# A four-layer graph network on one core: the last layer's edge pass as a walk over edge groups and node blocks, and another order of fronts in the projections

## The reference, cut to what matters

```
hn  = relu(layernorm(x))                      # the same norm ahead of every layer
msg = (hn @ weight[r] + bias[r])[src]         # r = edge type, 0 to 3
agg = segment_max(msg, dst, 6250)             # a node without edges gets 0
x   = x + agg + hn @ weight[4] + bias[4]
```

## Time and profile before

| | before |
|---|---|
| median of 3 runs | 5873.08 us |
| profiled execution | 5876.16 us, span 5874.4 us |
| PE busy | 3278.1 us (56%) |
| DVE | 2906.4 us (49%) |
| ACT | 1827.9 us (31%) |
| POOL | 3903.4 us (66%) |
| mean granted clock of TensorE | 0.728 |
| the last edge pass, first gather to the end of the span | 4816.0 to 5874.4 |
| of it behind the last scanned chunk | 5804 to 5874.4 |

### The profile page before, as it was taken

One profiled execution on the slowest core, in us unless ns is written; L12 is line 12 of the kernel. 1 busy time (PEld: TensorE's weight loads), 2 busy tenths in 40 slices (PEclk: granted clock), 3 DMA queues, 4 the chain that ended last, 5 costly groups with the idle time before them and its releaser, 6 DMA issues. The chain is left out here.

```text
span 5874.4 us, 89970 instructions
## 1 busy us (share of the span) xinstructions
PE 3278.1 (56%) x15772; PEld 2756.8 (47%) x15773; DVE 2906.4 (49%) x7625; ACT 1827.9 (31%) x6493; POOL 3903.4 (66%) x4083
## 2 busy tenths in 40 slices
PE   3444555545555525889999894244555563334332
PEld 3444455444555523677777644233445533333331
DVE  4233344434455656788888852344555652222221
ACT  2111111111122213666666653233344441111110
POOL 4777777677777747777776003777777517777776
PEclk9667777766677756999999995566677785555555
DMA  4222222211111112344444211222222134444443
GB/s 122 61 62 63 63 65 66 72 53 52 53 53 52 53 41 78 111 113 117 119 117 113 95 46 31 52 53 54 53 53 52 38 111 130 133 132 130 131 133 107
DMA packets 441899, 474.71 MB, mean 81 GB/s; under 512 B 131954, under 2 KB 337214, under 8 KB 441695
## 3 DMA queue, kind: packets, MB, share of 16 engines
q0 software_dynamic: 130464, 264.37, 17.1%
q1 hardware_dynamic: 184116, 146.31, 8.3%
q10 hardware_dynamic: 127227, 63.09, 3.6%
HBM read 315.46 MB, written 157.97 MB: 81 GB/s over the span
## 5 line engine op out<-in xcount | busy, mean ns | idle before, releaser
L1194 PE MATMUL pa<-arena,weighted 128*128 x4480 | 860.0, 367 | 855.8 <-POOLq L913 511.2
L1194 PEld LDWEIGHTS pa<-arena,weighted 128*128 128x128 f32 x4480 | 795.4, 273 | 909.4 <-issue 909.2
L422 POOL DMA_INDIRECT arena<-y_tab,slot x784 | 739.8, 944 | 398.7 <-issue 209.4
L1607 POOL DMA_INDIRECT arena<-t_tab,src_idx x784 | 777.5, 992 | 265.7 <-issue 216.0
L919 POOL DMA_INDIRECT arena<-h_tab,src_idx x784 | 742.8, 947 | 308.1 <-issue 221.9
L2490 POOL DMA_INDIRECT arena<-t_tab,src_idx x784 | 753.3, 961 | 244.9 <-issue 224.6
L919 POOL DMA_INDIRECT arena<-sage_tab,src_idx x784 | 739.8, 944 | 262.4 <-issue 216.1
L471 DVE TENSOR_TENSOR_SCAN scan_t<-mask,scan_t,pa 128x512 f32<-128x512 bf16 x196 | 250.9, 1280 | 737.1 <-PE pa L495 737.1
L495 PE MATMUL pa<-ident,arena 128*128 128x128 f32 x784 | 218.3, 434 | 603.9 <-DMA arena<-y_tab,slot 603.9
L495 PEld LDWEIGHTS pa<-ident,arena 128*128 128x128 f32 x784 | 140.1, 217 | 681.9 <-DMA arena<-y_tab,slot 430.8
L2731 PE MATMUL pa<-weighted 128*128 128x130 f32 x2240 | 422.6, 364 | 21.0 <-ACT weighted L2809 11.0
(11 more groups left out here) (522 smaller groups left out, 6559.9 us busy)
## 6 DMA issues: line engine op xcount, KB each, us to landing
gat_tab<-out_rows SPq DMA_DIRECT2D x248, 260.0 KB
scan_rows<-out_rows ACTq DMA_DIRECT2D x196, 256.0 KB, 3.7
arena<-t_tab,src_idx POOLq DMA_INDIRECT x1568
mask<-cut_row SPq DMA_DIRECT2D x196, 128.0 KB, 3.1
arena<-h_tab,src_idx POOLq DMA_INDIRECT x784
arena<-sage_tab,src_idx POOLq DMA_INDIRECT x784
y_tab<-arena SPq DMA_DIRECT2D x49, 256.0 KB, 2.3
arena<-y_tab,slot POOLq DMA_INDIRECT x784, 2.8
```

The source lines that it names most:

```text
L422: nc.gpsimd.indirect_dma_start(out=rows(c, t), out_offset=None, in_=table[:, :], in_offset=bass.IndirectOffsetOnAxis(ap=slot[:, c, t:t + 1 ...
L1194: ins = nc.tensor.matmul(pa[:, b * CE:b * CE + RW], hot[b][:, t * P:(t + 1) * P], ring[:, bass.ds(start + t * RW, RW)], start=(t == 0), st ...
L1607: nc.gpsimd.indirect_dma_start(out=rows[:, g % QR * QT + t, :], out_offset=None, in_=t1_tab[:, :], in_offset=bass.IndirectOffsetOnAxis(ap= ...
```

## The change

**The last pass** becomes a walk of the same 160 steps. `edge_pass`, `gather_results`, `scan_rows`, `last_idx`, `slot` and the rows of zeros go. POOL gathers by group into the ring of 8 groups, straight from `y_idx`; a group's slot is free when its last step has been staged. Tables in the pass's head: SP reads the destinations, DVE multiplies dst + 1 with the flag of each node's last edge (`last`), SP writes this to `last_rows`, POOL fetches it by step after group 2 (two gathers of 128 rows of 896), and PE and DVE turn it into a new `rel`, in which an edge is zero or negative unless it is the last of its node in the step's block. Then for step s, with b = s % 2:

- ACT `stage_group`: copy the 7 tiles out of the ring; `load_mask`: DMA of the cuts of the group to all partitions
- PE `turn`: 7 transposes; DVE `scan` over 896 edges, and two single-column operations for the carry (if the next step has the same group, the carry stays as it was, else it is the last column)
- PE `back`: 7 transposes; ACT `keep_back`: copy of 896 columns
- DVE `build`: one-hot of last edges; PE `select`: 7 products of `hot` with the kept rows, summed in PSUM, which pick each node's last row or zero
- DVE `add` to the block's rows of x; ACT `store`: DMA of the block to `out` (every step, also where the block goes on; the last 106 rows are stored by SP at the end)

**The projections.** Product banks are two again of one PSUM tensor. PE does turn(i+1) and ACT keep(i+1) ahead of group i's tiles. DVE does front(i+2) ahead of post(i) in all three, so the first two make three norms before their first post. Other edits: four memsets and one load of the setup go, some tables of the four-head pass get tensors of their own (`group_col1`, `block_col1`), and the last indices are no longer computed.

```diff
@@ project, DVE
-                        if left > 1 and starts is None:
+                        if left > 1:
                             front(dve, i + 2)
                         dve.wait_ge(group_product.sem, group_product.past(i + 1))
                         post(dve, i, b)
-                        if left > 1 and starts is not None:
-                            front(dve, i + 2)
@@ project, PE multiply and step
-                                if t == 4 and left > 0:
-                                    turn(i + 1)
-                                pe.wait_ge(tile_out.sem, tile_out.by_last_lap(i * NG + (max(t, 1) if t < 3 else max(t - 1, 2))))
-                                to = banks[t % 4][:, 0:n]
+                                pe.wait_ge(tile_out.sem, tile_out.by_last_lap(i * NG + (t + 1 if t > 1 else 2 - t)))
+                                to = pb[:, t % 2 * CE:t % 2 * CE + n]
...
-                        if left > 0 and by_tile is None:
+                        if left > 0:
                             turn(i + 1)
-                        multiply(i, b, left)
+                        multiply(i, b)
@@ project, ACT step
-                        if left > 0 and by_tile is None:
+                        if left > 0:
                             keep(i + 1, 1 - b)
...
-                                if t == 4 and left > 0:
-                                    keep(i + 1, 1 - b)
@@ the last pass
-        edge_pass(y_tab, D, y_idx, cut_row, ALU.add, ALU.max)
@@ the last pass: POOL, SP, DVE, PE, ACT
+                for g in range(GN):
+                    if g >= RG:
+                        pool.wait_ge(group_freed.sem, group_freed.past(g - RG + 1))
+                    for t in range(GT):
+                        nc.gpsimd.indirect_dma_start(
+                            out=edge_rows[:, g % RG * GT + t, 0:D], out_offset=None, in_=y_tab[:, :],
+                            in_offset=bass.IndirectOffsetOnAxis(ap=y_idx[:, g * GT + t:g * GT + t + 1], axis=0)
+                        ).then_inc(group_gathered[g % RG].sem, 16)
+                    if g == LAP:
+                        pool.wait_ge(stored.sem, stored.past(16))
+                        for k in range(2):
+                            nc.gpsimd.indirect_dma_start(out=rel_rows[k], out_offset=None, in_=last_rows[:, :],
+                                                         in_offset=bass.IndirectOffsetOnAxis(ap=group_col[:, k:k + 1], axis=0)
+                                                         ).then_inc(table_rows.sem, 16)
+                    if g > 0:
+                        landed(g - 1)
+                landed(GN - 1)
...
+                with sp.Fori(0, GN) as g:
+                    n = sp.value_load(retire_walk[0:1, bass.ds(g, 1)], min_val=1, max_val=SN)
+                    wait_apart(sp, edge_staged.sem, edge_staged.past(n))
+                    sp.sem_inc(group_freed.sem, 1)
...
+                def scan(s, b):
+                    after(dve, edge_turned, s + 1)
+                    after(dve, mask_loaded[b], (s - b) * 8 + 16)
+                    after(dve, edge_back, s - 1)
+                    after(dve, carry_ready, s)
+                    v.tensor_tensor_scan(run_t[b], mask_t[b], turned_ps[b], carry_t[b], ALU.add, ALU.max).then_inc(edge_scanned.sem, 1)
+                    after(dve, edge_scanned, s + 1)
+                    v.tensor_scalar(held_at, run_t[b][:, GE - 1:GE], of_step(on_flags, s + 1), None, ALU.mult).then_inc(carry_held.sem, 1)
+                    after(dve, carry_held, s + 1)
+                    v.scalar_tensor_tensor(out=carry_t[1 - b], in0=carry_t[b], scalar=of_step(same_flags, s + 1), in1=held_at,
+                                           op0=ALU.mult, op1=ALU.add).then_inc(carry_ready.sem, 1)
+                def build(s, b):
+                    after(dve, block_summed, s - 1)
+                    at = rel[:, s * GT:(s + 1) * GT] if isinstance(s, int) else rel[:, bass.ds(s * GT, GT)]
+                    v.tensor_tensor(hot[b].rearrange("p (t n) -> p t n", n=P),
+                                    iota_f[:, 1:P + 1].unsqueeze(1).broadcast_to([P, GT, P]),
+                                    at.unsqueeze(2).broadcast_to([P, GT, P]), ALU.is_equal).then_inc(hot_built.sem, 1)
+                def add(s, b):
+                    j = block_of(dve, s, b)
+                    row = x[:, bass.ds(j, 1), :].rearrange("p j d -> p (j d)")
+                    after(dve, block_summed, s + 1)
+                    after(dve, block_added, s)
+                    after(dve, block_stored, s * 16)
+                    v.tensor_tensor(row, row, last_ps[b], ALU.add).then_inc(block_added.sem, 1)
+                def body(i, b):
+                    if inside(i):
+                        scan(i, b)
+                        build(i, b)
+                    if inside(i - 2):
+                        add(i - 2, b)
...
+                def turn(s, b):
+                    after(pe, edge_staged, s + 1)
+                    after(pe, edge_scanned, s - 1)
+                    for t in range(GT):
+                        ins = nc.tensor.transpose(turned_ps[b][:, t * P:(t + 1) * P], staged_t[b][:, t * P:(t + 1) * P], ident[:, :])
+                    ins.then_inc(edge_turned.sem, 1)
+                def back(s, b):
+                    after(pe, edge_scanned, s + 1)
+                    after(pe, edge_kept, s)
+                    for t in range(GT):
+                        ins = nc.tensor.transpose(back_ps[:, t * P:(t + 1) * P], run_t[b][:, t * P:(t + 1) * P], ident[:, :])
+                    ins.then_inc(edge_back.sem, 1)
+                def select(s, b):
+                    after(pe, edge_kept, s + 1)
+                    after(pe, hot_built, s + 1)
+                    after(pe, block_added, s - 1)
+                    for t in range(GT):
+                        ins = nc.tensor.matmul(last_ps[b], hot[b][:, t * P:(t + 1) * P], kept_t[b][:, t * P:(t + 1) * P],
+                                               start=(t == 0), stop=(t == GT - 1))
+                    ins.then_inc(block_summed.sem, 1)
+                def body(i, b):
+                    if inside(i + 1):
+                        turn(i + 1, 1 - b)
+                    if inside(i - 1):
+                        select(i - 1, 1 - b)
+                    if inside(i):
+                        back(i, b)
...
+                def stage_group(s, b, start, need):
+                    after(act, edge_turned, s - 1)
+                    wait_apart(act, group_landed.sem, group_landed.past(need))
+                    nc.scalar.copy(staged_t[b].rearrange("p (t d) -> p t d", d=D),
+                                   ring[:, bass.ds(start, GT * RW)].rearrange("p (t w) -> p t w", w=RW)[:, :, 0:D]
+                                   ).then_inc(edge_staged.sem, 1)
+                def load_mask(s, b, need):
+                    after(act, edge_scanned, s - 1)
+                    act.dma_start(mask_t[b], cut_row[0:1, bass.ds((need - 1) * GE, GE)].broadcast_to([P, GE])).then_inc(mask_loaded[b].sem, 16)
+                def keep_back(s, b):
+                    after(act, edge_back, s + 1)
+                    after(act, block_summed, s - 1)
+                    nc.scalar.copy(kept_t[b], back_ps).then_inc(edge_kept.sem, 1)
+                def store(s, b, j):
+                    after(act, block_added, s + 1)
+                    act.dma_start(out[bass.ds(j * P, P), :], x[:, bass.ds(j, 1), :].rearrange("p j d -> p (j d)")
+                                  ).then_inc(block_stored.sem, 16)
+                STEP = [(0, NT - 2), (0, (RG - 1) * GT * RW), (1, GN)]
+                def body(i, b):
+                    if not isinstance(i, int) or 0 <= i < SN + 2:
+                        j, start, need = window_values(mybir.EngineType.Activation, scalar_walk, i, 0, STEP)
+                    if inside(i):
+                        keep_back(i, b)
+                    if inside(i - 2):
+                        store(i - 2, b, j)
+                    if inside(i) and inside(i + 2):
+                        stage_group(i + 2, b, start, need)
+                        load_mask(i + 2, b, need)
```

More of the change, by code:

```diff
@@ L125, in build @@
 def build(nc, a, out):
[L126 removed]
+    assert NT % NG == 0 and GN % RG == 0
     groups = NT // NG
@@ L250, in build @@
         sums_ready = count("sums_ready")
-        gathered = [count(f"gathered{c}") for c in range(NB)]
-        idx_staged = count("idx_staged")
+        iota_made = count("iota_made")
         hot_made = [count(f"hot_made{a}", 2 * LQ) for a in range(2)]
@@ L319, in build @@
         cuts_kept = count("cuts_kept")
[L320 to L325, removed]
+        edge_staged = count("edge_staged")
+        edge_turned = count("edge_turned")
+        edge_scanned = count("edge_scanned")
+        edge_back = count("edge_back")
+        edge_kept = count("edge_kept")
+        carry_held = count("carry_held")
+        carry_ready = count("carry_ready")
```

(26 more changed lines are left out.)

310 lines of the change are left out of this document (107 added, 203 removed).

## The result

The changed kernel takes 5939.75 us (median of 4 runs, 5926.5 to 5944.01) against 5872.95 (4 runs): ratio 1.0109, 95% interval 1.0092 to 1.0127. Forecast were 5850 and "faster"; it is 67 us slower. The time lies in the wide range of 5795 to 5965, but on the other side of no change, between the two prices of rival (b) (5910, and 5975 for both of its halves). That the range holds it is no merit of the mechanism that was forecast.

The account below looks back on a forecast made before the run. POOL's gathers bound the last pass's first half, the PE-ACT step its second: 533 + 516 + 14 + 2.5 = 1066 us, 7 more than now; projections gain 30; sum -23, 5850 us, range 5795 to 5965.

Parts of the forecast that it names:

- rival (b): Last pass: longer PE-ACT circle, by store in series (T 6.7) or clock 0.75 (6.6); 5910, both 5975; chance 0.28.
- Projections, -30: The three projections, with fronts ahead of posts, gain 14, 13 and 3 us, together 30, bounds 15 and 42.
- so I take 0.87: 3.3 / 0.87 = 3.8: Last pass: PE's granted clock taken as 0.87, so its 3.3 us full-level block takes 3.8 and a step 6.0.
- The circle: Last pass: PE's block, then ACT's keep(i) and stage(i+2), which turn(i+2) awaits: 3.3 + 2.2 us at full clock.
- ACT's part, 2.2: Last pass: ACT's two copies and the hand-overs, while PE stops, take 2.2 us a step, bounds 1.9 and 2.9.
- T: Time of one step of the last pass, forecast as 6.0 us.
- 980 us at 1.25: Last pass: POOL's 784 gathers keep their pace of one every 1.25 us, 980 us in all.
- 533 us to the 61st group: Last pass: the first 427 gathers, at 1.25 us each, take 533 us, before 86 steps of 6.0.
- POOL idle there for want of freed groups: Sign of being right: POOL waits for freed groups in the last half of the last pass.
- a clock under 0.8 in the last half: Sign of being wrong: granted clock under 0.8 in the last half of the last pass.
- scans waiting for masks: Sign of being wrong: the last pass's scans wait for masks, whose loads are issued two steps ahead.
- (c): Rival, last pass: transposes don't raise PE's clock; 0.70 to 0.75, steps 6.6 to 6.9, total 5910 to 5935; chance 0.10.

Follow-up runs that it names:

- experiment 1: The kernel before with the projection edits alone (front(i+2) ahead of post(i), two banks, turn and keep ahead of the tiles): 5853.4 us, ratio 0.9958.
- experiments 5 and 6: The changed kernel with unused PE work behind back(i), in PE's pause: seven transposes (5837.15 us), or four f32 products in their place (5841.9 us).
- experiment 7: The changed kernel without the store in each step or the addition's wait for it; SP stores all blocks at the end: 5950.71 us, ratio 1.0131.
- experiment 2: The changed kernel with the one-hot build reading its row from PSUM, select's results in one bank and select(s) behind add(s-1): 5952.45 us, ratio 1.0129.
- 3 to 4: From the changed kernel with ACT's stage(i+2) and mask load ahead of keep(i) and store (5844.86 us) to that plus the build from PSUM (5806.07).
- experiment 4: The changed kernel with both the build's row read from PSUM and stage(i+2) with its mask ahead of keep(i) on ACT: 5806.07 us, ratio 0.9882.

## Why the prediction was wrong

The sum was -23 us against the run of before; measured is +67 between the medians and +68 between the profiled runs.

- **Projections, -30: right in total, in part by luck.** -29.2 at the first gather, -24 of it by experiment 1. By part, from the last gather of the pass ahead to the first of the pass behind: the first gained 9.0 (127.0 to 118.0 us; 14 forecast), with posts 7.3 us apart; the second gained 19.2 (13 forecast), with posts 9.6 apart and not 10.9; the third gained 1.6 of 3. Beside them 3.8 were lost within the four-head pass, and 3.2 gained in the walks and the two-head pass, for which the prediction had nothing. Its errors offset each other.
- **"so I take 0.87: 3.3 / 0.87 = 3.8": the step that failed first.** The circle and its full-level block of 3.3 us were right; the clock put into it was not. The block takes 4.95 us in 67 of 83 steps and 4.63 on average. The mean clock of the pass was 0.76 to 0.79, near the walk's value that rival (b) used, and by 0.79 the block would be 4.2. The rest comes of dividing by a mean at all: it counts the pause, where the clock stood at 1.00 and nothing ran, while in the long blocks it was worth 3.3 / 4.95 = 0.67. The "unbroken and longer" bursts, taken as a help, were offset by a pause of 2 us in each step, and experiments 5 and 6 show that it was the pause.
- **ACT's part, 2.2: slightly high.** 1.93 to 2.04, since stage begins with keep's end. With it T is 6.9 to 7.0 with a long block and 5.2 to 5.6 with a short one, 6.58 over the pass's last 85 steps, from 5375.1 to 5934.6. Rival (b) was right in sign and place and in its clock half, whose T was 6.6 (4.4 + 2.2, measured 4.6 + 2.0); its other half, the store in series, is refuted (experiment 7). It had nothing for the gathers, and so 5910 and not 5940.
- **"980 us at 1.25", and so "533 us to the 61st group": wrong, the second step that failed.** A gather that starts in the first 0.7 us of a build takes 0.6 us more on average; the 107 of over 1.2 us lose 65 us in all, and 429 gathers took 568 us. The prediction took the build's price from the walk without seeing that its row read `pd`, PSUM, as one input, and that the diff's build reads `iota_f`, SBUF. The range had no term for it.
- **"POOL idle there for want of freed groups": wrong.** It waited 7.7 us in all. Slowed gathers and slow steps ran nearly abreast, and the groups still in the ring of 8 were worked off behind the last gather, in 100 us. Of the signs of being wrong, a clock under 0.8 in the last half and scans waiting for masks both came; the second cost nothing.
- **The sum redone:** 567 to the 61st group (533 forecast), 560 for the last 85 steps (516 for 86), 29 around them (16.5): 1156 against 1066, the whole miss of 90. The steps make 44 of it, the gathers 34.
- **(c), transposes don't raise the clock: refuted,** though its price (T of 6.6 to 6.9, up to 5935) came close. Seven transposes in the pause hold it at 0.98, four products too. The Trainium skill ("TensorE: Matmul & The Clock Gate", Part 4, PE-mode transpose) says that the full rate doesn't engage in transpose mode; these runs disagree for f32 transposes among products. What a kernel of transposes alone does, no run here shows.

What the two errors weigh depends on their order. With the step as it is, curing the gathers gave nothing (experiment 2, whose edit has its own price); with the circle cured (5845), it was worth 39 us more (3 to 4). On top of the cured clock (5837) it wasn't tried.

## What to carry to other kernels

Where two engines hand work round in a circle, write the circle down and ask which of its members could be issued one place earlier in its engine's stream: two calls moved on ScalarE were worth 95 us, more than the 55 that the pass was ever to gain. The pause of TensorE in this circle cost twice, as a pause and as clock in the work behind it. So where a circle has such a pause, price the work at the lower level, look for ways to fill the pause, and don't divide by the mean clock. When a cost is taken from a row of another stage, compare the operands too, memory by memory.

## What was unexpected of the hardware

- A VectorE operation on two SBUF inputs (the 1.09 us build) delays the gather of POOL that starts beside it: 1.2 to 1.85 us instead of 0.94, in all 107 cases of over 1.2 us to 0.82 us behind the operation's end. With one of the inputs in PSUM, 784 gathers took at most 0.96 us (experiment 4). The Trainium skill ("SBUF — State Buffer", Who interferes with whom) has the first half, that such an operation contends with GpSimd's reads, and infers that a DMA issued by GpSimd is not stalled by it, since making its descriptors needs the write side; these gathers were held up all the same.
- The granted clock can be high in the pause and low in the burst, 1.00 for 1.8 us without work, 0.52 through the 2.9 us of select behind the next turn. It was 1.00 in the pauses of all 83 steps counted, and 67 blocks took 4.95 us for work that takes 3.31 at the full level. With the pause filled, by transposes or by products, 78 blocks took 3.31.
- Two chips differ by 27% on one kernel (5873 and 7478 us), with the same durations for the scan, the build, ACT's copies and an undisturbed gather.
